# Attention with the values stationary in eight 64x32 tiles of TensorE, the probabilities streamed, and the results turned twice

## What is computed

```
scores = Q K^T / sqrt(16)        # 512 x 64, the second layer also masked
attn   = softmax(scores)         # over the 64 context tokens
out    = attn V                  # 512 x 16
y      = x + concat(out) Wo + bo
```

## Time and profile before

| what | value |
|---|---|
| median of 3 runs | 2354.14 us (2351.86 to 2357.58) |
| the profiled execution's own time | 2351.78 us |
| its span in the profile | 2349.9 us |
| TensorE matmuls busy | 2185.0 us, 93% of the span |
| VectorE / ScalarE / GpSimd busy | 62% / 37% / 15% |
| mean granted clock of TensorE | 0.969 of full |

### The profile page before, as it was taken

The page is one execution under the profiler, slowest core; times in us unless marked ns, Lnnn a source line. Parts: engine busy times, 40 slices in busy tenths (PEclk is TensorE's granted clock), DMA queues, the critical chain, the costliest instruction groups (busy, mean ns, idle before and its releaser), DMA issues. The chain is left out here.

```text
span 2349.9 us, 40584 instructions
## 1 busy us (share of the span) xinstructions
PE 2185.0 (93%) x15349; PEld 1868.5 (80%) x15349; DVE 1452.4 (62%) x3161; ACT 871.0 (37%) x1243; POOL 359.8 (15%) x346
## 2 busy tenths in 40 slices
PE   6999998739999959999998999999999999999998
PEld 4888887427888837777777888888888888888887
DVE  6888887775554357877776854544545454454444
ACT  3555554134544325555544322222222222222222
POOL 3111110106666411111111200000000000000000
PEclk9999999759999969999999999999999999999999
DMA  3122211104444311211114100000000000000000
GB/s 97 55 77 64 73 63 55 21 30 110 101 99 68 41 41 55 71 62 57 68 68 134 31 21 27 28 28 27 28 28 22 6 28 27 28 28 27 28 10 10
DMA packets 109098, 114.01 MB, mean 49 GB/s; under 512 B 16064, under 2 KB 97728, under 8 KB 108992
## 3 DMA queue, kind: packets, MB, share of 16 engines
q1 hardware_dynamic: 96704, 95.44, 12.8%
q0 software_dynamic: 12288, 17.05, 4.3%
HBM read 61.87 MB, written 50.59 MB: 48 GB/s over the span
## 5 line engine op out<-in xcount | busy, mean ns | idle before, releaser
L2205 DVE TENSOR_TENSOR zmix_hid<-zmix_act_gate,psum 128x1024 f32<-128x1024 f32 x128 | 156.3, 1221 | 379.3 <-issue 351.5
L2161 ACT ACTIVATE zmix_hid_hi<-zmix_hid 128x1024 fp32r<-128x1024 f32 x128 | 135.6, 1059 | 391.6 <-PE psum L144 250.7
L2153 ACT ACTIVATE zmix_act_gate<-psum 128x1024 f32<-128x1024 f32 x128 | 131.5, 1028 | 379.3 <-PE psum L144 379.3
L752 PE MATMUL psum<-att_v_cur,att_probs 128*128 128x96 f32 x2048 | 247.9, 277 | 3.3 <-ACT att_probs L911 3.1
L752 PEld LDWEIGHTS psum<-att_v_cur,att_probs 128*128 128x128 f32 x2048 | 238.3, 192 | 11.4 <-ACT att_probs L911 4.0
L2210 DVE TENSOR_TENSOR zmix_hid_lo<-zmix_hid,zmix_hid_hi 128x1024 fp32r<-128x1024 f32 x128 | 157.8, 1233 | 134.2 <-ACT zmix_hid_hi L2161 133.2
L142 PE MATMUL psum<-zmix_wd_hi,zmix_hid_hi 128*128 128x256 f32 x768 | 217.3, 283 | 2.2 <-DVE zmix_acc L2196 1.9
L143 PE MATMUL psum<-zmix_wd_lo,zmix_hid_hi 128*128 128x256 f32 x768 | 217.2, 283 | 0.0
L144 PE MATMUL psum<-zmix_wd_hi,zmix_hid_lo 128*128 128x256 f32 x768 | 217.1, 283 | 0.0
L2196 DVE SCALAR_TENSOR_TENSOR zmix_acc<-psum,opened_weight,zmix_acc 128x256 f32<-128x256 f32 x512 | 211.8, 476 | 1.6 <-PE psum L144 1.6
L911 ACT ACTIVATE att_probs<-psum 128x512 f32<-128x512 f32 x256 | 132.3, 603 | 144.0 <-PE psum L731 73.5
(11 more groups left out here) (387 smaller groups left out, 5443.2 us busy)
## 6 DMA issues: line engine op xcount, KB each, us to landing
x<-att_x_new SPq DMA_DIRECT2D x32, 512.0 KB, 2.9
att_x_in<-in_x SPq DMA_DIRECT2D x16, 512.0 KB, 3.8
rows<-att_normed_new SPq DMA_DIRECT2D x16, 512.0 KB, 3.0
att_x_in<-x SPq DMA_DIRECT2D x16, 512.0 KB, 3.8
turned<-att_newT SPq DMA_DIRECT2D x16, 512.0 KB, 2.8
zmix_acc<-x SPq DMA_DIRECT2D x16, 512.0 KB, 4.3
out_x<-zmix_acc SPq DMA_DIRECT2D x16, 512.0 KB, 3.2
moe_wd<-in_w_down SPq DMA_DIRECT2D x8, 768.0 KB, 5.4
```

The costliest lines, as they stand in the source:

```text
L752: m = pe.matmul(psum[:, 6 + t % 2, cols], probs[:, j, t * P:(t + 1) * P], v_cur[:, p, cols], start=True, stop=True)
L2153: act.activation(act_gate[:, :, :], psum[:, 0:2, :], ACT.Silu).then_inc(gate_out, 1)
L2161: act.activation(hid_hi[:, e % 2, :, :], hid[:, :, :], ACT.Copy).then_inc(hi_made, 1)
L2205: dve.tensor_tensor(hid[:, :, :], act_gate[:, :, :], psum[:, 2:4, :], ALU.mult).then_inc(up_out, 1)
```

## The change

The values become the stationary operand and the probabilities the moving one. Each head has a tile of the array of its own: 64 rows (its keys) by 32 columns (16 features, the ones column, and zeros). Four pairs of heads, that is eight tiles, fill the array, so that a batch has two groups (r = 0, 1) of eight matmuls with 512 columns each. The result has features on partitions and must be turned for the division: ScalarE copies it from PSUM to `av_raw` (`values_copy`), TensorE turns it (`turn_values`), VectorE divides (`normalise`, now twice a batch with 32 denominators and 512 results), and `turn_attention` turns it back. `maxima` reduces two 128-token tiles at once (128 x 1024). The copy of the turned maxima goes from VectorE to ScalarE. The order of the heads in `att` changes, and the rows of Wo are laid out to match before the launch (`by_half`). The orders in the bodies and the waits follow.

```
-        kv["v"] = sc.sb("v_aug", [P, B, NP, 2 * VW])
+        kv["v"] = sc.sb("v_aug", [P, B, NP, SLOT])
-        kv["wr"] = sc.sb("wr_sb", [P, KC, PE_COLS])
+        kv["wr"] = sc.sb("wr_sb", [P, KC, SLOT])
-        att = sc.sb("att", [P, TT, D])
+        av_raw = sc.sb("av_raw", [P, KC, 2, S])
+        by_row = av_raw[:, 1, 1, 0:P]
+        att = av_raw[:, :, 0, :].rearrange("p c (t d) -> p c t d", d=P)
```

`SLOT` is 32. The parts of TensorE:

```
             def maxima(b, p, c):
+                pe.wait_ge(q_hi, done(KC, b, c + 1))
                 if c == 0:
-                    pe.wait_ge(q_hi, done(KC, b, KC))
...
+            def weighted_values(b, p, r):
+                pe.wait_ge(exp_done, done(NP, b, (r + 1) * PAIR_ROWS))
+                if r == 0:
                     pe.wait_ge(v_ready, b + 1)
                     after(pe, x_ready, done(KC, b, 0))
+                else:
+                    pe.wait_ge(av_copied, done(2 * KC, b, 2))
+                pe.sem_inc(av_begun, 1)
+                for a in range(2):
+                    keys = slice(a * SK, (a + 1) * SK)
+                    for q in range(PAIR_ROWS):
+                        j = r * PAIR_ROWS + q
+                        m = pe.matmul(psum[q * SLOT:(q + 1) * SLOT, 6 + a, :], v_cur[keys, p, j, :], probs[keys, j, :], start=True, stop=True)
                 m.then_inc(av_made, 1)
+            def turn_values(b, r):
+                pe.wait_ge(av_copied, done(2 * KC, b, 2 * r + 2))
+                if r == 0 and there(b + 1):
+                    pe.wait_ge(q_lo, done(KC, b + 1, KC))
+                elif r == 0:
+                    pe.wait_ge(a_lo, done(KC, b, 0))
+                for a in range(2):
+                    for t in range(TT):
+                        m = pe.transpose(psum[:, 6 * r + t // 2, (t % 2 * 2 + a) * P:(t % 2 * 2 + a + 1) * P], av_raw[:, r, a, t * P:(t + 1) * P], ident[:, :])
+                m.then_inc(av_turned, 1)
             def turn_attention(b):
-                pe.wait_ge(av_taken, done(TT, b, TT))
+                pe.wait_ge(av_taken, done(KC, b, KC))
...
                 scores(b, p, 1)
+                weighted_values(b, p, 0)
                 if nxt:
                     queries(b + 1, 1 - p)
-                for t in range(TT):
-                    weighted_values(b, p, t)
-                    if t == 2 and there(b - 1):
-                        turn_new(b - 1, 1 - p)
-                    if nxt and t % 2 == 0:
-                        maxima(b + 1, 1 - p, t // 2)
-                if there(b - 1):
-                    route(b - 1, 1 - p)
-                turn_attention(b)
-                if there(b - 1):
-                    turn_logits(b - 1)
-                if nxt:
-                    turn_maxima(b + 1)
+                    maxima(b + 1, 1 - p, 0)
+                weighted_values(b, p, 1)
+                turn_values(b, 0)
+                turn_values(b, 1)
+                if there(b - 1):
+                    pe.wait_ge(av_taken, done(KC, b, 1))
+                    turn_new(b - 1, 1 - p)
+                if nxt:
+                    maxima(b + 1, 1 - p, 1)
+                turn_attention(b)
+                if there(b - 1):
+                    route(b - 1, 1 - p)
+                if nxt:
+                    turn_maxima(b + 1)
+                if there(b - 1):
+                    turn_logits(b - 1)
```

Of ScalarE:

```
+            def values_copy(b, r):
+                act.wait_ge(av_made, done(KC, b, r + 1))
+                after(act, a_turned, b)
+                after(act, lg_turned, b - 1)
+                for a in range(2):
+                    act.activation(av_raw[:, r, a, :], psum[:, 6 + a, :], ACT.Copy).then_inc(av_copied, 1)
+            def maxima_copy(b):
+                act.wait_ge(max_turned, b + 1)
+                after(act, st_made, done(NP, b, 0))
+                act.activation(maxT[:, :], psum[:, 7, :], ACT.Copy).then_inc(max_ready, 1)
...
                 exps(b, range(4, 8))
+                values_copy(b, 0)
                     queries_hi(b + 1, 1 - p)
+                values_copy(b, 1)
...
                     new_copy(b - 1, 1 - p)
+                attention_hi(b)
                     logits_rows(b - 1)
-                attention_hi(b)
+                    maxima_copy(b + 1)
```

Of VectorE:

```
-                for t in tiles:
-                    s = psum[:, 2:2 + PAIR_ROWS, t * P:(t + 1) * P].rearrange("p j (a k) -> p j a k", a=2)
-                    dve.tensor_reduce(s_max[:, t, :, 2 * c:2 * c + 2], s, AX.X, ALU.max).then_inc(s_taken, 1)
+                s = psum[:, 2:2 + PAIR_ROWS, half * 2 * P:(half + 1) * 2 * P].rearrange("p j (t a k) -> p t j a k", a=2, k=SK)
+                dve.tensor_reduce(s_max[:, 2 * half:2 * half + 2, :, 2 * c:2 * c + 2], s, AX.X, ALU.max).then_inc(s_taken, 1)
...
+            def normalise(b, r):
+                dve.wait_ge(av_turned, done(KC, b, r + 1))
+                av = psum[:, 6 * r:6 * r + 2, :].rearrange("p k (n c) -> p (k n) c", c=SLOT)
+                dve.reciprocal(recip[:, r, :], av[:, :, DH]).then_inc(av_recip, 1)
+                dve.wait_ge(av_recip, done(KC, b, r + 1))
+                dve.tensor_tensor(att[:, r, :, :].rearrange("p t (n c) -> p (t n) c", c=DH), av[:, :, 0:DH],
+                                  recip[:, r, :].unsqueeze(2).to_broadcast([P, NT // 2, DH]), ALU.mult).then_inc(av_taken, 1)
...
-                for t in range(TT):
-                    normalise(b, t)
-                    if nxt:
-                        maxima(b + 1, t // 2, [2 * (t % 2), 2 * (t % 2) + 1])
+                for r in range(KC):
+                    if nxt:
+                        maxima(b + 1, 0, r)
+                    normalise(b, r)
                 if nxt:
-                    maxima_copy(b + 1)
+                    for r in range(2):
+                        maxima(b + 1, 1, r)
```

More of the change, by code:

```diff
@@ L266, in clear @@
         pool.wait_ge(v_cleared, 1)
[L267 to L270, removed]
+        pool.memset(kv["v"][:, :, :, DH:DH + 1], 1.0).then_inc(v_cleared, 1)
+        pool.wait_ge(v_cleared, 2)
     def turn_context(pe):
@@ L709, in turn_maxima @@
             def turn_maxima(b):
-                pe.wait_ge(s_taken, done(TT * KC, b, TT * KC))
-                after(pe, av_taken, done(TT, b - 1, TT))
+                pe.wait_ge(s_taken, done(2 * KC, b, 2 * KC))
+                after(pe, av_taken, done(KC, b - 1, KC))
                 for t in range(TT):
@@ L737, in scores @@
                         pe.matmul(out, const["keysel"][keys, :, :], mask_cur[keys, p, :], start=False, stop=True).then_inc(st_made, 1)
-            def weighted_values(b, p, t):
-                if t == 0:
-                    pe.wait_ge(exp_done, done(NP, b, NP - 1))
+            def weighted_values(b, p, r):
+                pe.wait_ge(exp_done, done(NP, b, (r + 1) * PAIR_ROWS))
+                if r == 0:
                     pe.wait_ge(v_ready, b + 1)
                     after(pe, x_ready, done(KC, b, 0))
[L744 to L749, removed]
-                        pe.wait_ge(exp_done, done(NP, b, NP))
-                    cols = slice(j * 2 * VW, j * 2 * VW + PE_COLS)
-                    m = pe.matmul(psum[:, 6 + t % 2, cols], probs[:, j, t * P:(t + 1) * P], v_cur[:, p, cols],
-                                  start=True, stop=True)
-                m.then_inc(av_made, 1)
+                else:
[6 more added lines that the diff above has]
+                        m = pe.matmul(psum[q * SLOT:(q + 1) * SLOT, 6 + a, :], v_cur[keys, p, j, :], probs[keys, j, :], start=True, stop=True)
+                m.then_inc(av_made, 1)
@@ L883, in _ @@
             else:
-                pe.wait_ge(cleared, 2)
+                pe.wait_ge(cleared, 1)
                 turn_input(0, 0)
@@ L907, in exps @@
                 if 0 in pairs:
-                    after(act, av_made, done(TT, b, 0))
+                    after(act, av_made, done(KC, b, 0))
                 for j in pairs:
@@ L981, in _ @@
             input_norm(1, 1)
+            maxima_copy(0)
             batches(act, body, close)
@@ L1038, in queries_lo, with maxima @@
                                              qT_hi[:, p, m, :].bitcast(F32), ALU.add, ALU.subtract).then_inc(q_lo, 1)
-            def maxima(b, c, tiles):
-                if 0 in tiles:
+            def maxima(b, c, half):
+                if half == 0:
                     if c == 0:
@@ L1111, in body @@
                     between()
-                for t in range(TT):
-                    normalise(b, t)
-                    if ends and t == 0:
+                for r in range(KC):
+                    if nxt:
+                        maxima(b + 1, 0, r)
+                    normalise(b, r)
+                    if ends and r == 0:
                         inhibit()
@@ L1194, in _ @@
                         setup["values_out"](dve, b)
-                maxima(0, c, range(TT))
+                for half in range(2):
+                    maxima(0, c, half)
             if setup:
@@ L2317, in columns, with by_half @@
```

(2 more changed lines are left out.)

64 lines of the change are left out of this document (22 added, 42 removed).

## The result

The changed kernel takes 2339.72 us in the median of 5 runs (2335.36 to 2343.56), the kernel before 2351.86 us on the same chip: a ratio of 0.9938, 95% interval 0.9924 to 0.9951. The forecast was 2320. The sign is right; the gain is 0.6% where 1.4% was forecast, and the two layers went opposite ways. The profiled execution of the changed kernel is the fastest of its five, so the traces differ by 16.4 us where the medians differ by 12.1.

What follows compares the result with a forecast made beforehand. TensorE was taken to set the attentions' pace, VectorE close behind; afterwards a chain across engines. 15 x 0.7 + 15 x 1.6 = 34.5 us off 2351.78 is 2317, the median 2.4 above: 2320 us, range 2296 to 2350.

Steps and rivals of the forecast that it cites:

- TensorE's sum: TensorE's work in an attention batch: weighted values -7.75, groups +2.1, turns +1.75, tile-shape changes +0.2; -3.7 us a batch.
- Second layer: Second attention: period falls from 24.66 to 23.05 us a batch, -1.6 us, over 15 periods.
- the chain: Sequence of waits across engines in one batch, counted from the maxT write: closes at 21.65 us first layer, 23.05 second.
- the pass behind the copy: End of the second layer's batch: TensorE's pass after the turned-maxima copy at +22.9, giving period 23.05 us.
- First layer: First attention: period falls from 22.35 to about 21.65 us a batch, -0.7 us, over 15 periods.
- its wait on the previous batch ends as early; hidden: GpSimd in the attention batch: copies 256 instead of 272 values, and adds nothing to the period.
- Rival 3: TensorE's clock falls in the attention loop: half clock in one batch of ten, 2360 us and up; chance 0.05.
- one stretch of 10 us at 81% between the layers: Evidence used on rival 3: between the layers, TensorE at 81% kept clock 1.00, at 40% it fell to 0.71.
- The sum: Both attentions: 15 x 0.7 + 15 x 1.6 = 34.5 us off the profiled 2351.78, median 2320 us.
- Rival 1: Weighted-value groups: row halves take turns, 1.92 us a group, about 2370 us; chance 0.14 including its queue variant at 2347.
- Rival 2: Hand-overs in the new loop (or a 1.3 us group) cost 0.4 to 0.7 us a batch more, 2332 to 2345; chance 0.14.
- Rival 4: Batch chain shorter through ScalarE's order or quicker copies: further 0.5 to 1.5 us a batch off, 2275 to 2298; chance 0.07.

Runs made afterwards that it cites:

- GpSimd moved: Changed kernel with GpSimd's copy of the next values and two key products waiting for the previous batch's division, not its weighted values: 2321.89 us, ratio 0.9853.
- both: Changed kernel with GpSimd moved and eight extra bf16 matmuls filling TensorE's idle time in the first layer: 2311.43 us, ratio 0.9807.

## Why the prediction was right or wrong

**TensorE's sum: right.** A group was priced at 1.05 us and takes 1.09. Eight turns take 1.04 to 1.09 us at full clock, as before. In the second layer, at full clock, TensorE's busy time a batch fell from 0.98 x 24.66 = 24.2 to 0.914 x 22.83 = 20.9 us, 3.3 against the forecast 3.7; in the first layer, from 21.3 to 18.2 (GpSimd moved, a batch without a fall), 3.1. It doesn't set the pace any more.

**Second layer: right, and a little low.** Forecast 23.05 a batch and -1.6; measured 22.7 to 22.8 and -1.9. The steps of the chain hold within 0.2 us: counted from the end of the `maxT` write (1053.66), the masks and `maxima` end at +12.2 (forecast +12.2), the last two reductions at +21.4 (+21.55) and the copy at +22.8 (+22.9), and VectorE's last two reductions close the loop as it said. The last 0.15 us of the forecast, the pass behind the copy, doesn't belong to a period that starts at a copy's end.

**First layer: the chain was right, its conditions were not.** At full clock and with GpSimd out of the way the period is 21.7 us from pass to pass (GpSimd moved, batches without a fall) and 21.7 to 21.8 (both), against the forecast 21.65. In the kernel with both edits, counted from the pass at 240.64, the shift ends at +13.0 (forecast +12.9), the copy of the turned new rows at +18.1 (+18.05), the turned attention at +19.3 (+19.2), its copy at +20.4 (+20.3) and the router rows at +20.6 (+20.6). In the changed kernel two steps failed.

- *"GpSimd ... its wait on the previous batch ends as early; hidden."* The wait is on the weighted values, and these end earlier in the batch than before: the copy began 19.1 us after the `maxT` write, behind the last quarter, when VectorE took operands from PSUM; now it begins 12.3 us after it, amid the Newton steps. The step looked only at whether GpSimd would be late for others, not at whom it would run beside. It costs 0.9 us on the path to the shift; moving it is worth about 18 us in all (2339.7 to 2321.9, on different chips), with the clock that follows.
- *Rival 3, the clock, at one chance in twenty, "against: the gaps are 1.2 us at most".* The gap was 2.06 us, because the shift was late. But the argument fails without that too: with GpSimd moved the gaps are 1.09 to 1.27 us, about what was said, TensorE is busy 18.2 us in a batch of 21.7 at full clock (forecast 17.5 of 21.65), and the clock still fell in every second batch. The rival's price was wrong as well: it took one batch in ten to run at half clock throughout, at 14 us each. In the changed kernel the clock fell in the 13 steady batches of 15, each time for a part of the batch (6.8 us in the one shown), and a fall costs 1.0 to 1.5 us. What was wrong was to take one stretch of 10 us at 81% between the layers for proof. How busy TensorE is doesn't decide alone: in the kernel with GpSimd moved, batches with the same work alternate between keeping the clock and losing it. What else does, the runs don't settle.

The sum: 15 periods of the first layer were to give -10.5 us and gave +15.4; that is the whole miss and more, partly made up by 4 us in the second layer and 5 between the layers. The stretch between the layers took 475 to 481 us in all kernels of the study, with no edit there; what moves it was not looked into.

**The rivals.** Rival 1, in which the row halves take turns and a group takes 1.92 us, fell with the group's 1.09. Rival 2 (costlier hand-overs) has its total, 2332 to 2345, by accident: the second layer, with the same hand-overs, was below the forecast. (Its 0.4 to 0.7 us a batch over 30 periods would give 2332 to 2341, and rival 4's 0.5 to 1.5 would give 2275 to 2305; neither slip changes the account.) Rival 4 (a shorter chain) isn't seen in the changed kernel, but its place was named rightly: ScalarE's order in the tail was worth another 8 us.

## What to carry to other kernels

When the busiest engine gets lighter, ask two questions of what remains: which small work on the chain will now lie beside a GpSimd instruction, and whether TensorE still keeps its granted clock; here it lost it in batches whose longest waits were 1.1 us, and a measured clock, not the length of the gaps, is what tells. A wait of another engine that is tied to an event is moved along with that event; tie it to the moment at which its neighbour on VectorE reads PSUM. And a loop bound by hand-overs can be slower with less TensorE work: compare the granted clock before reading anything into a stage's time.

## What was not expected of the hardware

- VectorE's operations with two SBUF operands of 8 elements a lane took 0.35 to 0.54 us instead of 0.17 beside a GpSimd instruction, and ended with it. The Trainium skill (SBUF — State Buffer, Who interferes with whom) has this rule: a VectorE instruction with both inputs in SBUF and a GpSimd one that reads SBUF hold a pair of ports exclusively, and the other waits for the whole instruction. The trace agrees, 539 ns against 170.
- The granted clock fell in loops without any long gap: in every steady batch of the changed kernel's first layer, whose longest wait is 2.06 us, and in every second batch once GpSimd was moved, with no wait over 1.27 us. It settled into a rhythm with the batch: 23.9 us a period in the changed kernel's first layer, and the same 23.9 in the second once its masks were gone.
- Sixteen turns of 128x128 kept the clock as well as eight bf16 matmuls of the same length (0.99 and 0.97 in the two traces).
- Eight tiles of 64 rows by 32 columns run fully together in plain fp32: 16 instructions of 512 columns in 1.09 us.
